# The next unit's transposes and the last unit's inner products placed behind the projection, with shorter end and wider bias products

## The reference

```python
x = layer_norm(dense_t @ Wd.T, gd, bd)                       # 128 per sample
y = layer_norm(einsum('bnd,ed->bne', sparse_t, Ws), gs, bs)  # 26 rows x 128
y = einsum('bne,pn->bep', y, Wsi)                            # mix 26 rows into 32
y = swapaxes(layer_norm(y, gsi, bsi), 1, 2)
T = concatenate([x[:, None, :], y], axis=1)                  # 33 x 128
Z = einsum('bnd,bmd->bnm', T, T)                             # inner products
z = layer_norm(Z[:, TRIL_I, TRIL_J] @ Wl.T, gl, bl)          # first 384 of 512 kept
h = relu(concatenate([z, r_dense_t]) @ W_top1 + b_top1)
h = relu(h @ W_top2 + b_top2)
y = h @ W_top3
```

## Time and profile before

| | before |
|---|---|
| median of 3 runs | 175.03 us |
| lowest, highest | 173.59, 177.0 us |
| the profiled execution | 173.57 us |
| its span | 171.8 us |
| TensorE matmul busy | 83% |
| VectorE busy | 75% |
| ScalarE busy | 58% |
| GpSimd busy | 59% |

### The profile page before, as it was taken

How to read it: one execution, slowest core, us unless ns; L and a number is a source line. 1 busy time by engine, 2 the same in 40 slices (tenths; PEclk the granted TensorE clock), 3 DMA queues, 4 the chain that set the end, 5 groups by cost and what they waited for, 6 DMA issues and landing times.

```text
span 171.8 us, 4668 instructions
## 1 busy us (share of the span) xinstructions
PE 143.2 (83%) x1825; PEld 108.4 (63%) x1825; DVE 129.6 (75%) x300; ACT 99.4 (58%) x245; POOL 101.1 (59%) x111
## 2 busy tenths in 40 slices
PE   0179878798989946599999998969998899996995
PEld 0075543545559534467878685849695776886994
DVE  6359777796989498859899996949999877943151
ACT  0302344779765788667798686736676846721330
POOL 3777777777777777777777777777777200020000
PEclk9999999999999699879999999999999999999999
DMA  4833616133111113311111231111112200010000
GB/s 154 271 90 96 257 23 213 28 87 91 29 31 27 30 23 69 63 27 31 25 34 29 59 69 27 31 27 31 27 30 64 54 8 18 23 41 0 0 0 0
DMA packets 6003, 9.59 MB, mean 56 GB/s; under 512 B 2303, under 2 KB 3538, under 8 KB 5854
## 3 DMA queue, kind: packets, MB, share of 16 engines
q0 software_dynamic: 3392, 3.45, 11.0%
q1 hardware_dynamic: 2232, 5.08, 9.5%
q10 hardware_dynamic: 358, 0.78, 1.2%
HBM read 8.01 MB, written 0.00 MB: 47 GB/s over the span
## 4 chain that ended last, share of the span: by engine, by line
POOL 48%; PE 22%; issue 17%; DVE 5%; ACT 3%; DMA 2%; ACTq 1%; DVEq 0%
POOL g_sb L257 48%; PE psB L320 3%; PE psW L354 3%; PE psH L374 2%; PE psG L286 2%; PE psZ L335 1%; DMA g_sb<-in_table,row_id 1%; PE psZ L426 1%; PE psU L301 1%; PE psW L399 1%; DMA ids_sb<-in_ids 1%; ACT U L602 1%; ACTq L214 1%; DVE ssB L842 1%; DVE B L835 1%
## 5 line engine op out<-in xcount | busy, mean ns | idle before, releaser
L257 POOL DMA_INDIRECT g_sb<-in_table,row_id x104 | 99.7, 958 | 31.7 <-issue 31.4
L835 DVE TENSOR_TENSOR B<-psB,bias 128x512 f32<-128x512 f32 x31 | 20.0, 687 | 17.0 <-PE psB L320 16.9
L301 PE MATMUL psU<-wsi_x,g_sb 128*128 128x192 f32 (+4 forms) x128 | 21.3, 311 | 6.5 <-DVE g_sb L828 6.5
L301 PEld LDWEIGHTS psU<-wsi_x,g_sb 128*128 128x128 f32 x128 | 19.3, 193 | 10.1 <-DVE g_sb L828 10.1
L613 ACT ACTIVATE sqB<-B 128x512 f32<-128x512 f32 x31 | 19.1, 632 | 10.7 <-DVE B L835 10.5
L641 ACT ACTIVATE Zs<-psZ 32x264 f32<-32x264 f32 x59 | 22.3, 378 | 1.6 <-PE psZ L335 0.6
L320 PE MATMUL psB<-U,ws_g 64*128 64x512 f32 x64 | 19.9, 701 | 3.4 <-ACT U L602 3.3
L855 DVE TENSOR_TENSOR T<-B,psG 128x512 f32<-128x512 f32 x31 | 21.3, 687 | 1.1
L286 PEld LDWEIGHTS psG<-gram,sT 128*128 128x128 f32 x104 | 13.3, 197 | 13.7 <-ACT sT L589 10.8
L842 DVE TENSOR_REDUCE ssB<-sqB 128x16 f32<-128x512 f32 x32 | 21.7, 678 | 0.1
L286 PE MATMUL psG<-gram,sT 128*128 128x128 f32 x104 | 16.3, 297 | 0.7 <-ACT sT L589 0.7
(11 more groups left out here) (160 smaller groups left out, 217.2 us busy)
## 6 DMA issues: line engine op xcount, KB each, us to landing
g_sb<-in_table,row_id POOLq DMA_INDIRECT x104, 2.5
wl_sb<-in_wl SPq DMA_DIRECT2D x1, 1280.0 KB, 5.9
w_sb<-in_w SPq DMA_DIRECT2D x2, 512.0 KB, 5.4
w_sb<-in_w SPq DMA_DIRECT2D x1, 768.0 KB, 4.2
small_sb<-in_small SPq DMA_DIRECT2D x1, 615.5 KB, 3.7
dense_sb<-in_dense ACTq DMA_DIRECT2D x1, 512.0 KB, 7.2
Zt<-Zs SPq DMA_DIRECT2D x3, 80.0 KB
Zt<-Zs SPq DMA_DIRECT2D x3, 70.0 KB
```

What stands on the lines that cost most here:

```text
L257: pool.indirect_dma_start(g_sb[:, k, h * DSP:(h + 1) * DSP], None, table, bass.IndirectOffsetOnAxis(row_id[:, 2 * k + h:2 * k + h + 1], 0) ...
L301: mm = pe.matmul(psU[:, (lo - US * j) * PROJ:(hi - US * j) * PROJ], g_sb[:, SLOTS * b + c, :], wsi_x[:, c, lo - s0:hi - s0, :], start=(n = ...
L835: dve.tensor_tensor(B[:, h, :].rearrange("p (s j) -> p s j", j=PROJ), psB[h][:, :].rearrange("p (s j) -> p s j", j=PROJ), bias[:, :].rearr ...
```

## The change

In the steps 0 to 14 TensorE's order becomes `mix(t)`, `project(t)`, `transposes(t + 1)`, `inner(t - 1)`, `norms(t + 1)`, and only then the rest; step 15 is as before. ScalarE takes `prepare(t)` (work on weights, steps 1 to 8) ahead of `rows_out(t + 1)`. `bias_part` multiplies a bias column broadcast to 128 columns, and is spread over the steps 4 and 5; `shift_part` is spread over steps 1 to 3; the two VectorE pieces that read their results move to steps 4 and 6. At the end ScalarE takes `deviation_w(2)` ahead of its relay and issues one relay instead of two (GpSimd issues three); `third_layer2` runs whole before `last_linear`; VectorE adds the four squares, so that TensorE sums them with one product instead of four.

```diff
+def behind(u):
+    return u > 0
...
             pool.wait_ge(Z_kept, 4 * UNITS)
-            for q in (2, 6):
+            for q in (2, 4, 6):
                 relay(pool, LAST, q, 1, 2, d_zt_pool)
...
             def last_block():
+                third_layer2(2, K1)
                 pe.wait_ge(d_zt[LAST], 10 * 16)
-                pe.wait_ge(d_zt_act, 2 * 16)
-                pe.wait_ge(d_zt_pool, 2 * 16)
+                pe.wait_ge(d_zt_act, 16)
+                pe.wait_ge(d_zt_pool, 3 * 16)
                 pe.wait_ge(Z_kept, 4 * UNITS)
                 pe.wait_ge(sT_ready, UNITS)
                 last_linear(0)
-                third_layer2(2, K1)
...
                 top1(LAST, 0, psF[0][:, 0:BS])
+                top1(LAST, 1, psF[0][:, BS:2 * BS]).then_inc(h1_f, 1)
                 pe.wait_ge(W_sd, LAST)
-                for f in range(FLIN // P):
-                    pe.wait_ge(sq_f, f + 1)
-                    mm = pe.matmul(psV[:, 0:BS], ones_sb[:, :], z_sq[:, f * BS:(f + 1) * BS], start=(f == 0),
-                                   stop=(f == FLIN // P - 1))
-                mm.then_inc(W_summed, 1)
-                top1(LAST, 1, psF[0][:, BS:2 * BS]).then_inc(h1_f, 1)
+                pe.wait_ge(sq_added, 3)
+                pe.matmul(psV[:, 0:BS], ones_sb[:, :], z_sq[:, 0:BS], start=True, stop=True).then_inc(W_summed, 1)
...
-                        mm = pe.matmul(psH[:, f:f + 1], w1_sb[:, k, f * P:(f + 1) * P], bl_c[:, k:k + 1],
-                                       start=(k == 0), stop=(k == KZ - 1))
+                        mm = pe.matmul(psH[:, f * P:(f + 1) * P], w1_sb[:, k, f * P:(f + 1) * P],
+                                       bl_c[:, k:k + 1].broadcast_to([P, P]), start=(k == 0), stop=(k == KZ - 1))
...
                 mix(t)
-                if t + 1 < UNITS:
+                if t + 1 < UNITS and not behind(t + 1):
                     transposes(t + 1)
                 project(t)
+                if t + 1 < UNITS and behind(t + 1):
+                    transposes(t + 1)
+                    if t:
+                        inner(t - 1)
                 if t + 1 < UNITS:
                     norms(t + 1)
                 if late and j == 1 and t < UNITS - 1:
                     linear(b, EARLY[b], ALL)
-                if t:
+                if t and not (t + 1 < UNITS and behind(t + 1)):
                     inner(t - 1)
...
-                    shift_part(0, 2)
+                    shift_part(0, 1)
                 if t == 2:
-                    shift_part(2, CW)
+                    shift_part(1, 3)
                 if t == 3:
-                    bias_part()
+                    shift_part(3, CW)
+                if t == 4:
+                    bias_part(0, 2)
+                if t == 5:
+                    bias_part(2, K1)
...
                 keep_u(t)
-                if t + 1 < UNITS:
+                if t + 1 < UNITS and behind(t + 1):
+                    prepare(t)
                     rows_out(t + 1)
...
-                prepare(t)
...
             keep_z(UNITS - 1, 1)
+            deviation_w(LAST - 1)
             act.wait_ge(Z_kept, 4 * UNITS)
-            for q in (1, 4):
-                relay(act, LAST, q, 1, 2, d_zt_act)
-            deviation_w(LAST - 1)
+            relay(act, LAST, 1, 1, 2, d_zt_act)
...
-            relu2(LAST - 1)
             act.wait_ge(W_f, 4)
             act.activation(z_sq[:, 3 * BS:4 * BS], psU[:, 0:BS], ACT.Square).then_inc(sq_f, 1)
+            relu2(LAST - 1)
             deviation_w(LAST)
...
+                for n, f in enumerate((1, 2, 3)):
+                    dve.wait_ge(sq_f, 1 + f)
+                    if n:
+                        dve.wait_ge(sq_added, n)
+                    dve.tensor_tensor(z_sq[:, 0:BS], z_sq[:, 0:BS], z_sq[:, f * BS:(f + 1) * BS],
+                                      ALU.add).then_inc(sq_added, 1)
...
-                if t == 3:
+                if t == 4:
                     dve.wait_ge(m_done, 1)
...
-                if t == 4:
+                if t == 6:
                     dve.wait_ge(bz_done, 1)
-                    dve.tensor_tensor(b1_z[:, :], psH[:, 0:K1], b1_c, ALU.add).then_inc(bz_ready, 1)
+                    dve.tensor_tensor(b1_z[:, :], psH[:, 0:K1 * P:P], b1_c, ALU.add).then_inc(bz_ready, 1)
```

More of the change, by code:

```diff
@@ L200, in tower @@
                              "y_copied"))
+        sq_added = sem("sq_added")
         W_f, zT_f, sq_f, hd_scaled, h1_f, h1a_f, h1T_f, h2_f = (
@@ L483, in dense_part, with bias_part @@
                 mm.then_inc(hd_done, 1)
[L485 to L488, removed]
+            def bias_part(lo, hi):
+                if lo == 0:
+                    pe.wait_ge(d_w1, 16)
+                    pe.wait_ge(x1_ready, 1)
+                for f in range(lo, hi):
                     for k in range(KZ):
-                        mm = pe.matmul(psH[:, f:f + 1], w1_sb[:, k, f * P:(f + 1) * P], bl_c[:, k:k + 1],
-                                       start=(k == 0), stop=(k == KZ - 1))
-                mm.then_inc(bz_done, 1)
+                        mm = pe.matmul(psH[:, f * P:(f + 1) * P], w1_sb[:, k, f * P:(f + 1) * P],
+                                       bl_c[:, k:k + 1].broadcast_to([P, P]), start=(k == 0), stop=(k == KZ - 1))
+                if hi == K1:
+                    mm.then_inc(bz_done, 1)
             def shift_part(lo, hi):
@@ L732, in step @@
                 keep_u(t)
-                if t + 1 < UNITS:
+                if t + 1 < UNITS and behind(t + 1):
+                    prepare(t)
                     rows_out(t + 1)
+                elif t + 1 < UNITS:
+                    rows_out(t + 1)
+                    prepare(t)
                 else:
                     third_squares(0)
-                prepare(t)
                 if late and j == 3:
```

## The result

The changed kernel takes 182.0 us (median of 4 runs, 181.12 to 183.12) against 174.38 us of the kernel before in the same comparison: 4.6% slower, ratio 1.0463 with a 95% interval of 1.0409 to 1.0517. The profiled execution took 181.50 us, its span is 179.7 us instead of 171.8: 7.9 us more.

The account below looks back on a forecast made before the run. Gathers set the pace up to about 113 us, then the step loop and the end. Loop loss 6.5 less end gain 1.7 makes 4.8 us, forecast 179.1 us; own range 177 to 181.5.

Parts of the forecast that it names:

- the wide range: Whole kernel time: the range said to hold 8 in 10, from 174 to 183 us.
- rival 3: TensorE's clock falls in the new order: one or two falls at 1.7 us each, 181 to 183 us; chance 0.12.
- The step: Step loop: late norms delay `mult_a`, so a plain step takes 7.99 us, 0.92 longer.
- P: Start of the projection in a step; `mult_a` was forecast 3.28 us behind it instead of 2.36.
- The sum: First mix to the mix of step 15: 125.5 us, which puts that mix 6.5 us later.
- plain: Steps 1, 2, 4, 5, 6, 8, 9, 12, 13: taken at 7.99 us each, with no additions of their own.
- The clock: TensorE's granted clock: no fall taken for the new kernel, 1.00 between 54 and 59 us.
- The bias products' cover: Norms to next mix, 3.6 us, hides bias work of about 1.4 us a step; uncovered, `bias_part` costs up to 2.84.
- The end: Behind `variance(2)`: earlier root, fewer products of ones and the reordered last layers gain 1.7 us.
- Rival 1: Loop keeps up with the gathers, four steps within 32.5 us: 171.4 to 172.8 us; chance 0.17.
- Rival 2: Inner products hide wholly under the copy to sT and take 0.6 us: 176.2 to 177.6 us; chance 0.16.

Follow-up runs that it names:

- the kernel with step 5 filled: Changed kernel with the second half of the bias products run twice in step 5; 181.53 us, ratio 1.0479 to the kernel before.
- the kernel with four steps filled: Changed kernel with products run again over the same output in steps 1, 2, 4 and 5; 183.29 us, ratio 1.0585 to the kernel before.

## Why the prediction was right, and where its sizes were off

It forecast the sign, the cause and the place. The measured 182.0 us lies in the wide range, 2.9 us above the forecast; it is above the forecast's own range of 177 to 181.5 and in the band of rival 3 (181 to 183), which was given 0.12. The mechanism of the loss was right; the size came short in three steps, one of them through a fall of the clock. Step by step:

*The step.* Right. `mult_a` at P + 3.28 was forecast; in step 5 it came at P + 3.44, in steps with shorter inner products less. The hand-over, taken at about 0.05, was 0.04 from the norms (end 70.64) to `mult_a` (70.68). Mix to mix, forecast and measured: step 0 7.8 and 7.89; step 3 8.8 and 8.85; step 4 7.99 and 8.05; steps 7 and 11 9.9 and 9.8; step 10 8.6 and 8.55; steps 12 and 13 7.99 and 7.93 or less. Steps 10 and 14 came out (8.55 and 8.56) with some luck: the 8.6 was worked out from a step 14 of 7.94 us, by the 142.62 of the earlier trace rows; it lasted 142.45 - 134.68 = 7.77. Step 11 of the changed kernel, to be read beside the earlier trace rows:

```profile
121.05 0.66 PE L278 MATMUL psT<-small_sb,g_sb 128*128 128x128 f32 x4
121.64 0.77 PE L340 MATMUL psZ<-T 128*32 128x33 f32 x64
122.40 1.16 PE L291 MATMUL psG<-gram,sT 128*128 128x128 f32 x8
123.39 2.62 PE L359 MATMUL psW<-Zt,wl_g 127*128 127x128 f32 x22
126.70 1.16 PE L373 MATMUL psH<-z_sq,ones_sb 128*128 128x128 f32 x8 [0.69 <-ACT z_sq L659]
127.69 0.60 PE L306 MATMUL psU<-wsi_x,g_sb 128*128 128x160 f32 x3
```

No transposes wait for a gather here, and `variance` now waits 0.69 us for the square, with the inner products gone from the gap: both as told. From the norms to the next mix 5.29 us, 5.4 forecast.

*The sum.* 125.5 us from the first mix to that of step 15 was forecast, 128.14 measured. Three steps taken as plain were not. Step 2 (8.57): ScalarE's 0.68 us copy of x into Zt stands ahead of the copy of U; it was there before too, and the sum left it out: 0.6. Step 6 (9.40): the fall of the clock: 1.4. Step 9 (8.61): the inner products took longer than the bound allowed, 0.6:

```profile
103.81 0.55 PE L278 MATMUL psT<-small_sb,g_sb 128*128 128x128 f32 x3
104.28 1.46 PE L340 MATMUL psZ<-T 128*32 128x33 f32 x64
105.68 0.94 PE L291 MATMUL psG<-gram,sT 128*128 128x128 f32 x6
```

1.40 us from the first to the norms instead of 0.85; TensorE's weight loads paused for issue there, 0.24 and 0.20 us. Together 2.6 of the 2.64 missing; the other steps' differences cancel. The start came 0.38 us later by itself.

*The clock.* "I take no fall for the new kernel" is the step that failed. From 54 to 59 us the clock stood at 1.00, as forecast, but one fall came in step 6, which is the mechanism of rival 3 on top of the forecast, at 1.4 us. Rival 3's 1.7 us a fall was an estimate from the earlier trace rows, 5 x (1 - 0.66); no run shows a fall that cost 1.7, the traces showed 1.3 to 1.5. This fall stands behind an idle stretch (TensorE busy 0.00 of the us from 72 to 73), the one of the earlier trace rows behind a busy one: from 50 to 55 us TensorE was busy 0.99 or more of each us at a clock of 1.00, and from 55 the clock was 0.52 and 0.50. No run here shows why step 5, with an idle stretch as long ahead of it, had none.

Nor is it shown that the width of the bias products mattered: the kernel with the new end alone keeps the narrow ones (50.91 to 53.75 us), and its clock stood at 1.00 from 54 to 59 us as well (its stretch, columns as in the earlier trace rows):

```profile
54.00:59.00 5.00, 4.06 (x84) 2.83 (x83) 4.10 (x11) 4.57 (x9) 3.78 (x5) 1.00 0.14 26
```

And the kernel before had a second fall, far from the bias products, in the same step 6, which the prediction did not weigh (stretches):

```profile
71.00:72.00 1.00, 0.23 (x3) 0.00 (x0) 0.96 (x4) 0.60 (x1) 0.70 (x2) 1.00 0.17 35
72.00:73.00 1.00, 0.92 (x3) 0.69 (x5) 0.43 (x1) 0.41 (x2) 0.92 (x1) 0.55 0.20 33
73.00:74.00 1.00, 1.00 (x4) 0.00 (x0) 0.00 (x0) 0.91 (x3) 0.77 (x1) 0.50 0.21 31
```

*The bias products' cover.* Held: steps 4 and 5 are 0.06 and 0.15 us above the plain step.

*The end.* 1.7 us forecast, 1.7 measured. To be read beside the earlier trace rows, timeline of the changed kernel:

```profile
160.22 1.16 PE L373 MATMUL psG<-z_sq,ones_sb 128*128 128x128 f32 x8
...
161.41 0.37 ACT L674 ACTIVATE zsd<-psG,eps_c 128x128 f32<-128x128 f32 x1 [0.63 <-PE psG L373]
161.42 0.90 ACTq L219 DMA_DIRECT2D Zt<-Zs  x1
...
164.24 2.40 PE L404 MATMUL psW<-h1T,w_sb 128*128 128x128 f32 x16 [0.18 <-ACT h1T L797]
...
172.28 0.39 PE L451 MATMUL psG<-z_sq,ones_sb 128*128 128x128 f32 x2
...
174.70 0.49 PE L462 MATMUL psU<-h1T_last,w_sb 128*128 128x128 f32 x2
```

The root follows `variance(2)` at once. From the start of `variance(2)` to layer 2 it is 4.02 us (3.97 forecast, 5.62 before), from there to the last products 10.46 (10.55 forecast, 10.66 before).

*The rivals.* Rival 1, the loop keeping up with the gathers, fell: four steps take 34.7 us on the mean from step 7 to 14 (82.76 to 152.09, two blocks: 69.3), 34.5 forecast, above the 32.5 of the gathers. Rival 2 (inner products hidden under the copy) holds in part: putting them back behind the norms gave nothing that could be measured. Rival 3 holds in part too: one fall in the profiled execution, and mean granted clocks of 0.97 to 0.99 in all four.

## What to carry to other kernels

An order in which a wait on a transfer no longer blocks other work is worth nothing if the moved work was running inside another wait for free: ask what the moved instruction did in its old place before asking what it frees. Follow the loop from one start of the same instruction to the next, with the in-order queue of every engine, and compare its length with the pace of the source; here some 0.5 us of slack per step was all there was (an estimate: steps 7 to 10 before, 78.73 to 109.95 us, take 30.5 us without their waits for gathers of 0.35 and 0.38, against 32.5 for the gathers), and the move took 0.9. Two moves whose waits overlap need not add, so price them in all four combinations.

## What the runs showed of the hardware

One fall of the granted clock to 0.50 made its step 1.3 to 1.5 us longer (step 6: 9.40 with it, 8.11 without; step 2: 10.06 and 8.57), and it has no fixed place: it stood in step 6 in the changed kernel, in step 2 in the kernel with step 5 filled, and nowhere in the profiled execution of the kernel with the inner products behind the norms (clock 1.00, 180.76 us). These two falls stood behind stretches in which TensorE waited (busy 0.00 from 72 to 73 us in the changed kernel, 0.69 of the 2 us from 40 to 42 in the kernel with step 5 filled); the one of the earlier trace rows stood behind a busy stretch (0.99 or more of each us from 50 to 55), and a wait of the same 1.39 us ahead of step 5 brought none. What decides it is open. In the kernel before, the profiled falls cost nothing in the end, since waits for gathers came behind them (0.85 us at 72.08, 0.35 at 80.72).

The 64 inner products, always the same instructions, took from 0.62 us (step 14 before, up to the next work) to 1.40 us (step 9 after) and 1.56 us (step 5 of the kernel with four steps filled); these two long ones have pauses for issue in their weight loads, 0.24 and 0.20 us in the first, 0.43 and 0.20 in the second. What makes them pause is open.
